# Input projections in row pairs, gate and test moved to GpSimd, sums from a ones column, new orders, no unread products

## The reference, cut to what matters

```python
for i in range(2):                                   # Mamba blocks
    xz = rmsnorm(x) @ in_proj_w                      # 192 -> 2 x 384
    xr, res = split(xz)
    xr = silu(causal_conv4(xr) + conv_b)
    dt, B, C = split(xr @ x_proj_w)                  # 12, 16, 16
    delta = softplus(dt @ dt_proj_w + dt_proj_b)
    y = selective_scan(xr, delta, -exp(A_log), B, C) + xr * D
    x = x + (y * silu(res)) @ out_proj_w
q, k, v = heads(layernorm(x) @ w_qkv)                # 12 heads of 16
attn = relu(1 + s + s * s / 2), s = q k / 4;  attn = attn / sum(attn)
x = x + (attn @ v) @ w_proj + b_proj
x = x + bitlinear(silu(...) * ..., w_out)            # ternary weights, 8-bit rounded activations
```

## Time and profile before

| | us |
|---|---|
| Runs (3) | 413.19, 413.35, 414.96; median 413.35 |
| Profiled execution | 413.99, its span 412.2 |
| PE, PEld busy | 369.3 (90%), 201.4 (49%) |
| DVE, ACT, POOL busy | 320.7 (78%), 304.9 (74%), 200.1 (49%) |
| Granted TensorE clock, mean | 0.967 |

### The profile page before, as it was taken

The page is one execution under the profiler, slowest core; times in us unless marked ns, Lnnn a source line. Parts: engine busy times, 40 slices in busy tenths (PEclk is TensorE's granted clock), DMA queues, the critical chain, the costliest instruction groups (busy, mean ns, idle before and its releaser), DMA issues. The chain is left out here.

```text
span 412.2 us, 6636 instructions
## 1 busy us (share of the span) xinstructions
PE 369.3 (90%) x1882; PEld 201.4 (49%) x1882; DVE 320.7 (78%) x687; ACT 304.9 (74%) x574; POOL 200.1 (49%) x300
## 2 busy tenths in 40 slices
PE   0398998999999999999998898999999999999774
PEld 0233333345354453453634537865765665566553
DVE  3069898799999999989999898454678667577752
ACT  2257999899999989899979792347686777478541
POOL 5537345535435345353653445012447564558872
PEclk9999696899999999999999999699899999999999
DMA  6743000000000000000000000000000000000001
GB/s 149 196 149 72 6 0 2 1 1 2 0 1 2 0 1 0 2 1 0 2 2 0 2 1 2 2 2 0 2 2 13 19 11 2 12 21 21 21 17 33
DMA packets 6879, 7.91 MB, mean 19 GB/s; under 512 B 1566, under 2 KB 5623, under 8 KB 6840
## 3 DMA queue, kind: packets, MB, share of 16 engines
q1 hardware_dynamic: 5238, 5.71, 5.0%
q0 software_dynamic: 768, 1.57, 1.8%
q10 hardware_dynamic: 834, 0.17, 0.2%
HBM read 5.87 MB, written 1.57 MB: 18 GB/s over the span
## 5 line engine op out<-in xcount | busy, mean ns | idle before, releaser
L751 PE MATMUL bank<-ring,win 96*128 96x512 f32 x192 | 99.8, 660 | 2.5 <-issue 1.2
L1468 POOL TENSOR_TENSOR du<-dl,pair 128x512 f32<-128x512 f32 x24 | 30.5, 1273 | 72.2 <-DVE dmin L1793 72.2
L751 PEld LDWEIGHTS bank<-ring,win 96*128 96x128 f32 x192 | 37.0, 207 | 57.6 <-issue 50.5
L1786 DVE SCALAR_TENSOR_TENSOR pair<-bank,cw,pair 128x508 f32<-128x508 f32 (+2 forms) x72 | 52.3, 736 | 10.5 <-ACT pair L311 8.6
L1473 POOL TENSOR_TENSOR arena<-arena 128x512 f32<-128x512 f32 x24 | 30.5, 1272 | 29.2 <-DVE arena L1827 29.2
L877 PEld LDWEIGHTS bank<-wout,pair 128*128 128x128 f32 x192 | 32.6, 199 | 10.5 <-issue 9.8
L1462 POOL TENSOR_TENSOR arena<-arena,dl 128x512 f32<-128x512 f32 x24 | 30.5, 1270 | 14.2 <-DVE dl L1778 14.2
L877 PE MATMUL bank<-wout,pair 128*128 128x192 f32 x192 | 37.1, 347 | 0.0
L499 ACT ACTIVATE du<-bank 128x512 f32<-128x512 f32 x48 | 25.1, 597 | 15.0 <-PE bank L983 7.6
L805 PE MATMUL bank<-dbl,wdt 13*128 13x512 f32 x48 | 27.4, 655 | 4.3 <-issue 1.3
L1814 DVE TENSOR_TENSOR_SCAN arena<-arena 128x512 f32<-128x512 f32 x24 | 29.2, 1217 | 0.0
(11 more groups left out here) (183 smaller groups left out, 872.7 us busy)
## 6 DMA issues: line engine op xcount, KB each, us to landing
out<-h SPq DMA_DIRECT2D x16, 96.0 KB, 1.6
win<-in_w SPq DMA_DIRECT2D x2, 576.0 KB
arena<-ffn_in_t SPq DMA_DIRECT2D x1, 768.0 KB
wout<-out_w SPq DMA_DIRECT2D x2, 288.0 KB
arena<-ffn_out_t SPq DMA_DIRECT2D x1, 384.0 KB
wa<-w_qkv SPq DMA_DIRECT2D x1, 288.0 KB
wb<-w_qkv SPq DMA_DIRECT2D x2, 144.0 KB
h<-emb,idx POOLq DMA_INDIRECT x16, 6.5
```

Of the source, the lines that this page charges most:

```text
L751: last = nc.tensor.matmul(bank[:, b, :], win[:, j // NG, k, m * P:(m + 1) * P], xtr[:, j % 2, k, :], start=(k == 0), stop=(k == KH - 1))
L1468: nc.gpsimd.tensor_tensor(du[:, g, c, :], dl[:, g, c, :], xc[:, g, c, :], ALU.mult).then_inc(du_ready, 1)
L1786: nc.vector.scalar_tensor_tensor(acc, seqs(bank[:, X_BANKS[c], :])[:, :, 0:LEN - tap], cw[:, j // NG, c, TAPS - 1 - tap:TAPS - tap], acc, ...
```

## The change

Eight edits, in the order of the data:

1. The input projection is cut into 128 and 64 rows. Blocks go in pairs: the even one has rows 0 to 127 in the first product, the odd one rows 64 to 191; the missing 64 rows of both are two products in the two halves of the array. `turn_in` turns 128 columns twice (64 of them both times), and a block is complete only when its odd partner is done.
2. `gate` and `weakest_below` move from VectorE to GpSimd.
3. A column of ones is kept behind each block of squared scores; `values` multiplies 129 columns, so the sum of the values stands beside the product. `sum_tokens`, `sum_values`, `take_csum`, `spread_values` go. `take_sums` moves to VectorE and takes its addend from PSUM.
4. Queries, keys and values read their 64-row rests from the overlapping half of two 128-row transposes, so `take_x` copies two tiles instead of three.
5. All `keep_clock` calls go (the new constants are zero).
6. PSUM banks are given anew; for instance bank 4, which `turn_x` writes, now holds B spread over the partitions.
7. The loops of all engines have a new order. On ScalarE the three logarithms stand together, ahead of the branch and of `decays`.
8. `square_scores(0)` stands ahead of `states_act(7)`, and `turn_x(0)` waits for `bx_ready` 24, the last `input_times_b` of chunk 7.

```diff
             def in_columns(j, m):
+                first, second = IN_BANKS[m - m % 2], IN_BANKS[m - m % 2 + 1]
+                pe.wait_ge(xt_ready, 2 * j + 1 + m % 2)
...
-                for k in range(KH):
-                    last = nc.tensor.matmul(bank[:, b, :], win[:, j // NG, k, m * P:(m + 1) * P], xtr[:, j % 2, k, :],
-                                            start=(k == 0), stop=(k == KH - 1))
-                return last
+                nc.tensor.matmul(bank[:, IN_BANKS[m], :], win[:, j // NG, m * P:(m + 1) * P], xtr[:, j % 2, m % 2, :],
+                                 start=True, stop=False)
+                if m % 2:
+                    rest = win_rest[:, j // NG, m // 2 * P:(m // 2 + 1) * P]
+                    nc.tensor.matmul(bank[:, first, :], rest[64:P, :], xtr[64:P, j % 2, 1, :], start=False,
+                                     stop=True).then_inc(x_ready if m - 1 < CI else z_ready, 1)
+                    nc.tensor.matmul(bank[:, second, :], rest[0:64, :], xtr[0:64, j % 2, 0, :], start=False,
+                                     stop=True).then_inc(x_ready if m < CI else z_ready, 1)
...
+            def gate(j, c):
+                pool.wait_ge(scan_dve, (j + 1) * DECAYING * DVE_U)
+                pool.wait_ge(yv_done, 3 * j + c + 1)
+                pool.wait_ge(sz_ready, 3 * j + c + 1)
+                nc.gpsimd.tensor_tensor(xc[:, j % NG, c, :], sz[:, j % NG, c, :], yv[:, c, :],
+                                        ALU.mult).then_inc(gated, 1)
...
+            def take_sums(s):
+                if s == 0:
+                    dve.wait_ge(wx_ready, 3)
+                if s >= 2:
+                    dve.wait_ge(nm_turned, s - 1)
+                dve.wait_ge(pv_ready, CH * s + CH)
+                for c in range(CH):
+                    at = c * (P + 1)
+                    nc.vector.tensor_scalar(nm[:, s % 2, c, :], bank[:, PV_BANK, at:at + P],
+                                            bank[:, PV_BANK, at + P:at + P + 1], None, ALU.add).then_inc(nm_out, 1)
...
-            for i in range(10):
+            for i in range(12):
                 if i - 4 in CHUNKS:
+                    magnitude(i - 4, 0)
+                    exponential(i - 4, 0)
...
+                if i - 4 in CHUNKS:
+                    logarithm(i - 4, 0)
+                    positive_part(i - 4, 2)
                     logarithm(i - 4, 1)
+                    logarithm(i - 4, 2)
                 if i - 5 in CHUNKS:
                     states_act(i - 5)
                 if i - 4 in CHUNKS:
-                    positive_part(i - 4, 2)
                     decays(i - 4, 0)
...
-            pe.wait_ge(xt_ready, 16)
-            keep_clock(3, 1)
...
+            pe.wait_ge(sz_ready, 23)
+            pe.wait_ge(bx_ready, 24)
             turn_x(0)
```

More of the change, by code:

```diff
@@ L694, in _ @@
             take_attention(14)
-            take_hidden(9)
-            take_sums(15)
             take_input(12)
@@ L726, in weight_sums, with keep_clock @@
                     .then_inc(wtot_ready, 1)
+            def keep_clock(n, b):
+                for _ in range(n):
+                    nc.tensor.matmul(bank[:, b, 0:P], ident[:, :], ident[:, :], start=True, stop=True)
             def turn_in(j, k):
-                pe.wait_ge(xs_ready, j + 1)
                 if k == 0:
@@ L1246, in _ @@
+            turn_input(6)
+            pe.wait_ge(att_out, 9)
+            project(8)
+            pe.wait_ge(x_out, 8)
+            project_up(6)
+            pe.wait_ge(h_att, 9)
+            turn_sums(9)
+            pe.wait_ge(qxt_ready, 7)
+            project_down(3)
+            pe.wait_ge(nm_out, 30)
+            values(10)
             pe.wait_ge(h_out, 4)
             turn_hidden(4)
-            pe.wait_ge(y_done, 6)
-            turn_x(3)
-            pe.wait_ge(att_out, 9)
-            project(8)
@@ L1548, in hidden_step, with ones_scores @@
                                         ALU.mult).then_inc(deq2_ready, 1)
+            def ones_scores():
+                pool.wait_ge(scan_dve, 7 * DECAYING * DVE_U)
+                pool.wait_ge(t_ready, CI * 7)
+                pool.wait_ge(bx_ready, CI * 7)
+                for b in range(2):
+                    nc.gpsimd.memset(sq[b][:, :, :, P:P + 1], 1.0).then_inc(ones_sq, 1)
             def ones_columns(b):
-                chunks = (5, 7)[b]
+                chunks = (5, NJ)[b]
                 pool.wait_ge(scan_dve, chunks * DECAYING * DVE_U)
@@ L2125, in _ @@
-            memoryless_states(6, 0)
-            convolve(7, 2, 2)
-            input_times_b(6, 1)
-            convolve(7, 2, 3)
-            gate(5, 1)
+            states_dve(6)
+            add_h(5, 0)
+            add_h(5, 1)
+            input_times_b(7, 0)
+            delta(7, 1)
+            memoryless_states(7, 0)
+            scan_first(7, 0)
+            normalise(0)
             normalise(1)
-            scan_first(6, 0)
-            gate(5, 2)
-            skip(6, 0)
+            skip(7, 0)
@@ L2152, in _ @@
-            raise_flag(6)
-            variances(1)
-            error(7, 1)
-            states_dve(6)
-            delta(7, 0)
-            sum_tokens(0)
-            gate(6, 0)
-            error(7, 2)
-            delta(7, 1)
-            take_k(0, 0)
-            input_times_b(7, 0)
-            memoryless_states(7, 0)
-            input_times_b(7, 1)
-            gate(6, 1)
-            scan_first(7, 0)
-            gate(6, 2)
-            skip(7, 0)
-            scan_first(7, 1)
-            delta(7, 2)
@@ L2171, in _ @@
-            times_c(7, 0)
-            memoryless_states(7, 1)
-            take_k(0, 1)
-            times_c(7, 1)
-            input_times_b(7, 2)
-            memoryless_states(7, 2)
-            scan_first(7, 2)
-            skip(7, 1)
-            times_c(7, 2)
-            weakest_below(7)
-            add_h(6, 0)
+            delta(7, 2)
+            normalise(3)
+            memoryless_states(7, 1)
+            input_times_b(7, 1)
+            times_c(7, 0)
+            input_times_b(7, 2)
@@ L2182, in _ @@
+            variances(1)
+            scan_first(7, 1)
+            memoryless_states(7, 2)
+            times_c(7, 1)
+            normalise(4)
+            normalise(5)
+            skip(7, 1)
+            normalise(6)
+            take_k(0, 0)
+            normalise(7)
+            scan_first(7, 2)
+            times_c(7, 2)
+            take_k(0, 1)
             skip(7, 2)
-            add_h(6, 1)
             raise_flag(7)
             states_dve(7)
-            gate(7, 0)
-            gate(7, 1)
@@ L2371, in _ @@
-            round_input(12)
-            hidden_inverse(10)
+            largest_hidden(10)
+            divide(14)
+            input_inverse(13)
+            round_input(12)
+            hidden(11)
+            hidden_inverse(10)
+            round_hidden(9)
+            take_sums(15)
             add_attention(14)
```

1505 lines of the change are left out of this document (671 added, 834 removed).

## The result

The changed kernel takes 418.62 us (median of 8 runs, 414.16 to 421.38), the kernel before 413.3 beside it: a ratio of 1.0088, with an interval of 1.0057 to 1.0118. The ratio leaves out executions over 1.5% above the fastest of their kernel (here the one of 421.38). It got slower by 0.9%; the forecast was 394.4, 4.6% faster, within 388 to 401. The profiled execution took 418.15 us, its span 416.3, at a mean granted clock of 0.878 (before: 413.99, 412.2, 0.967).

The account below looks back on a forecast made before the run. Bound: three engines full together in Mamba laps, TensorE in the second stage, a chain at the end. Laps 9.5, change of stage 3, second stage 4, end 5.5 make 22 us, less 3 for waits: 394.4 us, range 388 to 401.

Parts of the forecast that it names:

- A lap of 25.3 us: Mamba stage: a lap falls 1.4 us to 25.3, giving 9.5 us over seven laps, bounds 0 and 15.
- I sum them as one resource: Mamba lap: VectorE's two-SBUF-operand instructions (9.9 us) and GpSimd's (14.6) exclude each other, sum 24.5, the highest of four.
- rival 2: Mamba laps: small GpSimd instructions hold VectorE off too, 26.4 a lap, 402 us; chance 0.27 together with rivals 3 and 4.
- Rival 1: Mamba laps: the clock falls in every lap from TensorE's gaps; 423 with all struck, priced at 417 us; chance 0.13.
- TensorE's term: Mamba lap: half products run in pairs, 2.3 us less, busy time from 26.3 to 24.0 us.
- Rival 4: Mamba laps: half products don't pair or form changes cost, lap gain gone, 404 us; chance 0.27 with rivals 2 and 3.
- ScalarE's term: Mamba lap: four table loads in place of five, 1.28 us less, busy time from 25.5 to 24.2 us.
- The change of stage: Between stages: 9.1 us hidden TensorE work lost against 7.3, 1.9 and 3.35 (clock); 3 gained, bounds -5 and +8.
- the 7.3 of wait taken as gained: Change of stage: ScalarE's 7.34 us idle before the first squares, behind chunk 7's branch, would be avoided.
- Second stage -4: Second stage: TensorE loses three sums of the values, 5.6 us, of which 4 are gained.
- end -5.5: End: unread products on the chain removed, 5.5 us gained; bounds 7.8 gained at full clock, 1.3 lost at the lower.
- Rival 5: Whole kernel: all bounds on the good side, 24.5 us a lap and the clock up, 383 us; chance 0.10.

Follow-up runs that it names:

- short gates: The run with the norm first, with the GpSimd gates computed over the first 64 of 512 columns only: 393.24 us, ratio 0.9513.
- the norm first: The wide run with GpSimd's scale and power for the next chunk's norm moved ahead of its second step-input product and second gate: 408.58 us.
- The wide run: The changed kernel with step products and those spreading B, B times C, and C over 77 or 128 rows, zeros in the rest: 409.04 us.
- the two runs with 10.8 us at half clock: The run with short gates (393.24 us), and the changed kernel with half the output product between the first two step products (413.91 us).
- early-change run: The norm first, plus last chunk's B in bank 2, so the second stage's first transposes start earlier, and four normalisations earlier on VectorE: 406.98 us.
- tests back: The run with the norm first, with the three one-column tests a lap back on VectorE for chunks 0 to 6: 413.33 us.

## Why the prediction was wrong

- **A lap of 25.3 us: wrong, for the undisturbed lap too.** The first wrong step is "I sum them as one resource": 9.9 us of VectorE and 14.6 of GpSimd, 24.5. The mechanism (exclusion) was right, but a sum takes for granted that each works while the other holds the port. VectorE keeps a list in order: while its `skip` waits for the port, its products from PSUM wait too. So the wait has to be added to the engine, not set beside it. Measured: VectorE is busy 26.3 of 26.6 us, and 24.3 of 24.5 with short gates. Of the 26.3, an estimated 3.6 us are stretch by the port; the 22.7 left are under the 23.6 of the prediction. The laps came to 26.8 (26.6 with the norm first), which is what rival 2 had as 26.4, but for another reason: `scale` and `power` first gave 0.2, and the tests nothing. Without most of the half clock the seven laps were 183.4 us, 4.7 less than before where 9.5 was forecast: these 4.8 us are this step's part of the miss in the laps, and the clock's is 9.1.
- **The clock: put at nothing in the sum, and it cost 9.1 us.** Rival 1 happened, and I gave it 0.13. "With TensorE as full as it will be" took busy time for what holds the clock. Half clock in the laps went from 17.1 to 54.6 us, in stretches of 6.8 and 10.2. The wide run brings the laps from 192.5 to 183.4 us: 9.1 us for 44 us less at half clock. I priced the case at 417 (by its own terms 416); 418.6 came. The price fits by luck in part: rival 1 has gaps of TensorE as the cause, and the wide run has more gaps and holds the clock; and it has nothing for the change of stage (4.0 lost) and for the longer lap at full clock.
- **TensorE's term held.** The pairs of halves run side by side, start within 0.01 us of each other (150.18 and 150.19 for L683 and L685), and TensorE is busy 23.98 us in lap 6 and 23.2 in the laps at full clock of the wide run; 24.0 was forecast. Rival 4 is refuted.
- **ScalarE's term held.** Four table loads of 1.28 us in the lap from 141.5 (141.66, 153.97, 157.71, 164.23), and 23.0 us busy in lap 6, 23.8 in the wide run, for 24.2.
- **The change of stage: wrong sign.** 4.0 us longer, inside the bound of +5. I weighed TensorE's hidden work against ScalarE's wait. The failed step is the 7.3 of wait taken as gained. The wait for the branch (7.34 us) did go, but it moved: ScalarE now waits 6.33 and 3.64 us for the queries and 1.95 before the first squares. The clock, which was to give 3.35, is at half for 23.9 us of this stage in place of 6.4. Given back later: by the early transposes 1.1 us, by unread products alone 0.5, by VectorE's order together with unread products 3.3. The copy of the keys stood ahead of the last scans in VectorE's list, which I had not looked at.
- **Second stage -4 and end -5.5: 3.3 came in all.** TensorE is busy 39.3 of 40 us from 300 on, for 38.4 in the earlier trace rows, so it is still the full engine there, and of the 5.6 us of the sums of the values only a part can have come. The end's 5.5 took for granted that most of the clock stays without the unread products: at full clock with them and at half without them it is as long, within 1.1 us, and in the two runs with 10.8 us at half clock in place of 23.4 it was 4.2 us shorter. The bounds (7.8 gained, 1.3 lost) held it. Rival 5 is mis-summed: all bounds on the good side give 380 and not 383.

The Trainium skill, "TensorE: Matmul & The Clock Gate", section "What's actually happening", says that the clock follows how busy TensorE has been. The traces agree for the wait of 9.7 us at the change of stage (242.66 to 252.37), in which the clock falls to 0.50 at 246.13. They differ in the laps, where it fell at 150.56 with TensorE busy all the time. The measurements decide: in this kernel the same number of products over more rows kept the clock where narrow ones lost it.

"SBUF — State Buffer", section "Who interferes with whom", of the Trainium skill also says that a `tensor_scalar` can run in a mode that takes the shared port. The 4.10 us for four normalisations in the early-change run agree with it.

Open: why the clock came back differently from run to run in the first two laps (7 to 31 us at half clock in them), why it held longer in the tail of two runs, how much of the change of stage is VectorE's order alone, and what order would spare VectorE the port without leaving the gate out.

## What to carry over

Where TensorE loses its clock though it is busy, look at the rows that its products use: a product of 13 or 16 rows could be run over 77 with zero weights in the same time, and that gave about 9 us in the changed kernel, where unread products gave nothing. It did not help over longer waits: with all products wide the clock still fell at waits of 1.6 and 3.7 us. And unread products are not useless everywhere: in the kernel before, taking them out cost 3.9 us. Where two engines share a port, don't add up their uses and compare; add the wait to the one that works in order, and ask what else stands in its list. And before moving work to an idle engine, look whether its operands lie in SBUF on both sides: here each 1.27 us of gate on GpSimd cost VectorE about 0.7.

## What was not expected of the hardware

- The clock fell with TensorE busy without a break, and held with gaps of 0.7 to 1.1 us three times a lap (wide run: laps 3 to 7 have one stretch of 3.4 us). With a gap of 1.6 us a lap (tests back) it fell at two of them.
- A product over 77 rows took what one over 13 took. The step products by line (ns min/median/max), in the changed kernel

```profile
L743 PE MATMUL bank<-dbl,wdt x48: 587/588/1056, 34.6 to 229.4; 13*128 13x512 f32 x48
```

and in the wide run:

```profile
L744 PE MATMUL bank<-dbl,wdt x48: 590/593/1057, 34.6 to 220.6; 77*128 77x512 f32 x48
```

- Small GpSimd instructions of one column took up to 1.87 us (3.48 for three) when VectorE's products of two SBUF operands went first; on VectorE the same tests changed no undisturbed lap.
- The clock of the tail differs between runs whose tails are the same program: 34.5 us at a mean of 0.66, 30.3 at 0.82.
